# Turning P on two row tiles of 64 rows, both halves of an item in one go

## The chip, the cores and the metric

The kernel runs on one core of a Trainium2 chip. The metric is the device time of one execution in microseconds; of the kernel before, three executions were timed and their median counts. The profile and the trace come from one further execution, taken by the hardware profiler.

## The reference

A block of 16 sequences of 128 tokens with 128 features passes a small cross attention and then six layers of windowed self-attention and a gated feed-forward net. Nearly all of the time goes into the six layers. What matters of one layer, cut from the reference:

```python
def attn_layer(x, Wqkv, qs, ksc, Wo):
    q, k, v = jnp.split(x @ Wqkv, 3, -1)          # 16 heads of 64
    q, k = l2norm(q) * qs, l2norm(k) * ksc        # then a rotary turn of both
    ...
    sim = jnp.einsum('bhwie,bhwje->bhwij', bq, bk2) * QK_SCALE   # windows of 32, with the one before
    sim = jnp.where(mask, -jnp.finfo(sim.dtype).max, sim)
    attn = jax.nn.softmax(sim, -1)
    out = jnp.einsum('bhwij,bhwje->bhwie', attn, bv2)
    return out @ Wo

def ffn_layer(x, g, bln, W1, b1, W2, b2):
    xn = (x - mu) / jnp.sqrt(var + 1e-05) * g + bln
    a, gate = jnp.split(xn @ W1 + b1, 2, -1)
    return a * jax.nn.gelu(gate, approximate=False) @ W2 + b2

for i in range(DEPTH):                            # DEPTH = 6
    x = attn_layer(shift_tokens(x), ...) + x
    x = ffn_layer(shift_tokens(x), ...) + x
```

The kernel calls the softmax's result P. To multiply it with the values on TensorE, P has to be turned (its keys must lie on partitions); the result is PT.

## The kernel before

An item is one sequence in one layer: 6 x 16 = 96 items, worked in 48 pairs. Every engine has one instruction stream, written out by hand in its `step`, and `pipeline` (L176) repeats that for one pair after the other. One pass of the loop works on three pairs at once: `on(0)` is the newest pair (its products with Wqkv), `on(1)` the one before (scores, softmax, values, output projection), `on(2)` the oldest (the feed-forward net). The last argument of most steps is the item of the pair, r = 0 or 1. The order inside `step` is fixed, and an engine that waits holds up everything behind it.

PSUM has eight banks of 512 columns, and `BANK_USERS` (L202) writes out who uses which bank in which order. Before a product is written, `freed` (through `bank_left`, L237) lets TensorE wait until the readers of that bank's last user are done; `FREED` (L192) names the semaphores of those readers. Three of the eight lists touch the change:

```python
[("chunk", 1, 0, 0), ("up", 0, 0, 2), ("v", 1, 0, 0), ("chunk", 1, 1, 0)],                     # bank 0
[("chunk", 0, 0, 0), ("turn_p", 0, 0, 1), ("chunk", 2, 0, 0), ("chunk", 3, 1, 0), ...],        # bank 2
[("turn_qk", 1, 1, 1), ("turn_p", 1, 0, 1), ("values", 0, 0, 1), ("chunk", 2, 1, 0)],          # bank 6
```

So the product `v_chunk(1, 0, 0)` goes into the bank that `up(0, 2)` held, whose reader is `gelu` on ScalarE (semaphore `gelu_done`, three activations, L628); and `chunk(2, 0, 0)` goes into the bank of `turn_p(0, 1, 0)`, whose reader is the copy `p_out(0, 1, 0)` (L588).

P of one item lies in two halves of eight heads each (e = 0, 1), each 128 rows by 512 columns. `turn_p(e, lag, r)` (L1060) turns one half by four transposes of 128 x 128 through the helper `turn` (L1007 to L1010) into one bank; `PT_full[e]` tells ScalarE, which copies the bank to PT (`p_out`, L588) and sets `PT_ready[e]`; `values` (L1066 to L1080) waits for both halves. A half can be turned when `divide` on GpSimd (L413) has set `P_ready[e]`.

The order on TensorE around the two turns of item 0 is: `scores(0, 1, 1)`, `up(2, 2)`, `turn_p(0, 1, 0)`, `v_chunk(1, 0, 0)`, `turn_p(1, 1, 0)`, `chunk(3, 0, 0)`, `chunk(2, 0, 0)`, `values(1, 0)`, `down(2)`. Around those of item 1 it is: `down(2)`, `turn_p(1, 1, 1)`, `chunk(1, 0, 1)`, `turn_p(0, 1, 1)`, `chunk(3, 0, 1)`, `chunk(2, 0, 1)`, `values(1, 1)`. On ScalarE the order around the copies of item 0 is `gelu(2)` with a table load before and behind it, `p_out(0, 1, 0)`, `p_out(1, 1, 0)`, `split_high`, `exp(1, 1, 1)`, `exp(0, 1, 1)`. A `chunk` or `v_chunk` is three products of 512 columns (L1003 to L1005, `product`).

`values` runs on four tiles of 64 rows by 64 columns of the array and `scores` on eight tiles of 64 by 32; everything else in the loop uses the whole array. At the very end of the program 32 products on two row tiles of 64 by 128 turn the result back (L1206).

Of the kernel before, what the change touches and what calls it, by code (L numbers as in the profile page):

```python
# [31 lines left out]
def program(nc, x, ctxT, Wqkv, Wo, W1, W2, by_feature, every_token, shape_consts, out):  # L32
# [8 lines left out]
    def sem(name):  # L41
        return es.enter_context(nc.semaphore(name))

    with es:
# [15 lines left out]
        maskf, ident, centring, mean_of = (sc[:, 128 * i:128 * i + 128] for i in (2, 3, 4, 5))  # L60
# [25 lines left out]
        P = sb("P", [128, 2, 2, 8, DH])  # L86
        PT = sb("PT", [128, 2, 2, 512])
# [41 lines left out]
        def sems(name, n):  # L129
            return [sem(name + str(k)) for k in range(n)]  # L130
# [2 lines left out]
        SP_SEMS = [vs_full, wo_loaded, w2_loaded, w1_loaded]  # L133

        ch_full, v_full, qkT_full, sc_full = sems("ch_full", 4), sems("v_full", 2), sems("qkT_full", 4), sems("sc_full", 2)
        PT_full, up_full, pv_full = sems("PT_full", 2), sems("up_full", 3), sem("pv_full")
        Wo_full, xc_full, var_full, y_full = (sem(s) for s in ("Wo_full", "xc_full", "var_full", "y_full"))
        PE_SEMS = (ch_full + v_full + qkT_full + sc_full + PT_full + up_full + [pv_full, Wo_full, xc_full, var_full, y_full])

        rot_done, ss_done, t2_done = sems("rot_done", 4), sems("ss_done", 4), sems("t2_done", 4)  # L140
        mx_done, sc_out, sum_done, rs_done = sems("mx_done", 2), sems("sc_out", 2), sems("sum_done", 2), sems("rs_done", 2)
# [28 lines left out]
        wait_met = sem("wait_met")  # L170


        def n_(n):
            return n + START
# [59 lines left out]
        def bank_of(kind, k=0, r=0):  # L234
            return K[bank_place(kind, k, r)[0]]
# [236 lines left out]
        def _(act):  # L472
# [24 lines left out]
            with act.Fori(0, NB // PAIR) as pair:  # L497
# [23 lines left out]
                for j in range(2):  # L521
                    act.wait_ge(c_hT, pair * 2 + j + 1 + START)
                    act.sem_inc(wait_met, 1)
                    for g in range(2):
                        p = slice(64 * g, 64 * g + 64)
# [4 lines left out]
            def step(it, on, splitting):  # L530
# [50 lines left out]
                    ps = P[:, r, e].rearrange("p g c -> p (g c)")  # L581
                    nc.scalar.activation(ps, ps, ACT.Exp).then_inc(exp_done[e], 1)

                def p_out(e, lag, r):
                    n = (it - lag) * 2 + r
                    act.wait_ge(PT_full[e], n_(n) + 1)
                    act.wait_ge(pv_full, n_(n) - 1)
                    nc.scalar.copy(PT[:, r, e], bank_of("turn_p", e, r)[:]).then_inc(PT_ready[e], 1)  # L588

                def o_out(h, lag, r):  # L590
                    n = (it - lag) * 2 + r
# [113 lines left out]
        def _(dve):  # L705
# [68 lines left out]
            def step(it, on, splitting):  # L774
# [38 lines left out]
                def minus_maxima(e, lag, r):  # L813
                    n = (it - lag) * 2 + r
                    dve.wait_ge(mx_done[e], n_(n) + 1)
                    dve.wait_ge(PT_full[e], n_(n) - 1)
                    nc.vector.tensor_tensor(P[:, r, e], by_head(bank_of("scores", e, r)[:], 8), spread(nm[:, r, e], 8, DH),
                                            ALU.subtract).then_inc(sc_out[e], 1)

# [130 lines left out]
        def _(pe):  # L950
# [42 lines left out]
            def step(it, on, splitting):  # L993

                def freed(kind, k=0, r=0):

                    for readers, value in bank_left(it, kind, k, r):
                        pe.wait_ge(readers, value)
# [8 lines left out]
                def turn(bank, src, done):  # L1007

                    for t in range(4):
                        i = nc.tensor.transpose(bank[:, 128 * t:128 * t + 128], src[:, 128 * t:128 * t + 128], ident[:])  # L1010
                    i.then_inc(done, 1)
# [45 lines left out]
                                            stop=True, skip_group_check=True)  # L1057
                    i.then_inc(sc_full[s], 1)

                def turn_p(e, lag, r):  # L1060
                    n = (it - lag) * 2 + r
                    pe.wait_ge(P_ready[e], n_(n) + 1)
                    freed("turn_p", e, r)
                    turn(bank_of("turn_p", e, r), P[:, r, e].rearrange("p g c -> p (g c)"), PT_full[e])

                def values(lag, r):  # L1066
                    n = (it - lag) * 2 + r
# [84 lines left out]
                    scores(0, 1, 1)  # L1152
                if on(2):
                    up(2, 2)
                if on(1):
                    turn_p(0, 1, 0)
                if on(0):
                    v_chunk(1, 0, 0)
                if on(1):
                    turn_p(1, 1, 0)  # L1160
                if on(0):
                    chunk(3, 0, 0)
                    chunk(2, 0, 0)
# [1 line left out]
                    values(1, 0)  # L1165
                if on(2):
                    down(2)
                if on(1):
                    turn_p(1, 1, 1)
                if on(0):  # L1170
                    chunk(1, 0, 1)
                if on(1):
                    turn_p(0, 1, 1)
                if on(0):
                    chunk(3, 0, 1)
                    chunk(2, 0, 1)
# [97 lines left out]
```

## Time and profile before

| | us |
|---|---|
| median of 3 executions | 1595.66 |
| lowest, highest of them | 1594.83, 1598.72 |
| the profiled execution, its own time | 1600.49 |
| its span, first to last instruction | 1598.6 |
| TensorE busy in the span | 1506.6 |
| VectorE busy in the span | 1399.6 |
| ScalarE, GpSimd busy in the span | 1175.3, 1168.4 |

The span is what the trace covers; about 1.9 us of the execution's time lie around it. A product's start in the trace is the time at which it was handed to the array; where the weights are not there yet the columns stream later, so the start of the next product, less one product's length, is the better mark for when a product really began.

### The profile page before, as it was taken

What the parts mean: (1) busy time and instruction counts of PE and PEld (TensorE: products, weight loads), DVE (VectorE), ACT (ScalarE), POOL (GpSimd) and SP (SyncE); (2) the same over time, 40 slices, a digit from 0 to 9 for tenths busy, and PEclk for the clock granted to TensorE, in tenths of its full rate; (3) what the DMA queues carried; (4) which work ended last, traced back from release to release, by engine and by line L of the source; (5) the groups of instructions that cost most, each with busy time, mean ns of one, the idle gap of its engine ahead of it and who ended that gap; (6) DMA issues with size and microseconds to landing.
All of it is one profiled execution on the core that took longest, in us unless ns stands there. A gap on an engine that the chain in (4) does not pass through costs nothing.

```text
span 1598.6 us, 80227 instructions
## 1 busy us (share of the span) xinstructions
PE 1506.6 (94%) x31136; PEld 1251.0 (78%) x31136; DVE 1399.6 (88%) x2545; ACT 1175.3 (74%) x2333; POOL 1168.4 (73%) x1118
## 2 busy tenths in 40 slices
PE   4589999999999999999999999999999999999996
PEld 3367888888888888888888888888888888888875
DVE  3587899999999999989999999999999999999982
ACT  3456687788778778778877877877877777777772
POOL 1276777878877887787787788788778777777760
PEclk8689999999999999999999999999999999999996
DMA  5110011011110111101112110111110101000010
GB/s 144 42 44 28 28 36 42 26 49 58 31 36 26 42 39 57 41 26 36 42 29 68 29 38 29 33 42 61 36 35 20 30 25 62 29 20 30 20 30 28
DMA packets 41462, 62.40 MB, mean 39 GB/s; under 512 B 3662, under 2 KB 30412, under 8 KB 41420
## 3 DMA queue, kind: packets, MB, share of 16 engines
q1 hardware_dynamic: 41420, 61.84, 13.2%
q8 instruction: 27, 0.44, 0.1%
q14 instruction: 15, 0.12, 0.0%
HBM read 18.84 MB, written 1.05 MB: 12 GB/s over the span
## 4 chain that ended last, share of the span: by engine, by line
PE 86%; issue 4%; ACT 3%; DVE 2%; ACTq 1%; POOL 0%; DVEq 0%; POOLq 0%
PE bank L1010 13%; PE bank L1080 12%; PE bank L1092 10%; PE bank L1003 9%; PE bank L1053 8%; PE bank L1004 8%; PE bank L1005 8%; PE bank L1127 5%; PE bank L1116 3%; PE bank L1035 3%; PE bank L1117 2%; PE bank L1118 2%; ACT v L576 2%; DVE xng L841 1%; PE bank L1106 1%
## 5 line engine op out<-in xcount | busy, mean ns | idle before, releaser
L393 POOL TENSOR_TENSOR u<-u,t 128x512 f32<-128x512 f32 x384 | 498.2, 1308 | 40.5 <-DVE t L802 40.5
L407 POOL TENSOR_TENSOR u<-u,rn 128x512 f32<-128x512 f32 x384 | 401.8, 1068 | 78.8 <-ACT rn L556 78.8
L413 POOL TENSOR_TENSOR P<-P,rs 128x512 f32<-128x512 f32 x192 | 196.5, 1045 | 172.6 <-DVE rs L826 172.6
L1003 PE MATMUL bank<-Wl,xsh 128*128 (+1 forms) x576 | 273.4, 475 | 26.1 <-ACT v L576 22.7
L802 DVE TENSOR_TENSOR t<-bank,TS 128x512 f32<-128x512 f32 x384 | 258.0, 682 | 28.1 <-ACT sq L545 25.5
L793 DVE TENSOR_TENSOR u<-bank,TC 128x512 f32<-128x512 f32 x384 | 261.9, 682 | 6.0 <-ACT sq L545 3.1
L786 DVE TENSOR_REDUCE ss<-sq 128x8 f32<-128x512 f32 x384 | 250.5, 673 | 6.4 <-ACT sq L545 6.4
L1004 PE MATMUL bank<-Wh,xsl 128*128 (+1 forms) x576 | 228.5, 397 | 0.0
L1005 PE MATMUL bank<-Wh,xsh 128*128 (+1 forms) x576 | 228.0, 396 | 0.0
L545 ACT ACTIVATE sq<-bank 128x512 f32<-128x512 f32 x384 | 218.9, 598 | 5.8 <-PE bank L1005 5.3
L1010 PE MATMUL bank<-shape_constants,u 128*128 128x128 f32 x1536 | 219.2, 275 | 3.4 <-POOL u L407 3.2
L1010 PEld LDWEIGHTS bank<-shape_constants,u 128*128 128x128 f32 x1536 | 182.2, 141 | 34.9 <-POOL u L407 5.0
L562 ACT COPY qT<-bank 128x512 f32<-128x512 f32 x192 | 115.2, 600 | 122.3 <-PE bank L1010 121.1
L1080 PEld LDWEIGHTS bank<-PT,vs 64*64 64x64 f32 x6144 | 163.9, 135 | 37.5 <-issue 37.5
L1080 PE MATMUL bank<-PT,vs 64*64 64x32 f32 x6144 | 187.8, 220 | 3.0 <-ACT PT L588 3.0
L1080 PE MATMUL bank<-PT,v 64*64 64x32 f32 x6144 | 186.1, 219 | 2.6 <-issue 2.6
L1092 PE MATMUL bank<-OT,WoS 128*128 128x256 f32 x768 | 175.5, 382 | 1.2 <-ACT OT L594 1.2
L1080 PEld LDWEIGHTS bank<-PT,v 64*64 64x64 f32 x6144 | 164.7, 135 | 2.8 <-issue 2.8
L1003 PEld LDWEIGHTS bank<-Wl,xsh 128*128 128x128 f32 x576 | 109.5, 190 | 62.5 <-issue 55.7
L1092 PEld LDWEIGHTS bank<-OT,WoS 128*128 128x128 f32 x768 | 143.4, 192 | 19.2 <-issue 1.3
L1053 PEld LDWEIGHTS bank<-kT,qT 64*32 64x32 f32 x12288 | 123.3, 105 | 32.3 <-issue 32.3
L594 ACT COPY OT<-bank 128x512 f32<-128x512 f32 x192 | 109.1, 594 | 45.4 <-PE bank L1080 45.4
(102 smaller groups left out, 3040.0 us busy)
## 6 DMA issues: line engine op xcount, KB each, us to landing
vs<-v SPq DMA_DIRECT2D x96, 384.0 KB, 3.3
Wraw<-in_L_ffn_Wqkv_dram SPq DMA_DIRECT2D x72, 117.5 KB, 2.1
WoS<-in_L_ffn_Wo_dram SPq DMA_DIRECT2D x6, 512.0 KB, 3.7
W1h<-Wh SPq DMA_DIRECT2D x6, 341.0 KB, 2.5
W1l<-Wl SPq DMA_DIRECT2D x6, 341.0 KB, 2.9
Wraw<-in_L_ffn_W_dram SPq DMA_DIRECT2D x12, 116.0 KB, 2.2
OT<-in_x_dram SPq DMA_DIRECT2D x2, 512.0 KB, 5.6
v<-in_ctx_dram SPq DMA_DIRECT2D x2, 512.0 KB, 6.9
```

The source lines that it names most:

```text
L393: nc.gpsimd.tensor_tensor(u[:, r, c], u[:, r, c], t2[:, r, c % 2], ALU.add).then_inc(add_done[c], 1)
L407: nc.gpsimd.tensor_tensor(by_head(u[:, r, c]), by_head(u[:, r, c]), spread(rn[:, r, HC * c:HC * c + HC], HC, DH), ALU.mult).then_inc(qk_re ...
L786: nc.vector.tensor_reduce(ss[:, r, HC * c:HC * c + HC], by_head(square_out(c, r)), AX, ALU.add).then_inc(ss_done[c], 1)
L793: nc.vector.tensor_tensor(by_head(u[:, r, c]), by_head(bank_of("chunk", c, r)[:]), TC[:, layer(it - lag), c % 2].broadcast_to([128, HC, DH ...
L802: nc.vector.tensor_tensor(halves(t2[:, r, c % 2]), halves(bank_of("chunk", c, r)[:])[:, :, ::-1, :], TS[:, layer(it - lag), c % 2].broadca ...
L1003: nc.tensor.matmul(out, x[0], Wl[:, w], start=True, stop=False)
L1004: nc.tensor.matmul(out, x[1], Wh[:, w], start=False, stop=False)
L1005: nc.tensor.matmul(out, x[0], Wh[:, w], start=False, stop=True).then_inc(done, 1)
L1010: i = nc.tensor.transpose(bank[:, 128 * t:128 * t + 128], src[:, 128 * t:128 * t + 128], ident[:])
L1053: i = nc.tensor.matmul(bank_of("scores", e, r)[64 * w2 + 32 * a:64 * w2 + 32 * a + 32, at + (32 if w == 0 else 0):at + 64], qT[f, s, t, 32 ...
L1080: i = nc.tensor.matmul(bank_of("values", h, r)[64 * e:64 * e + 64, 64 * t + 32 * w2:64 * t + 32 * w2 + 32], (vs, v)[w2][p, r, head:head + ...
L1092: i = nc.tensor.matmul(bank_of("Wo")[:, 0:2 * S], WoS[:, k], OT[:, k].rearrange("p r s -> p (r s)"), start=(k == 0), stop=(k == INNER // 1 ...
```

## The change

The two calls of `turn_p` for an item become one. It waits for both halves of P and for both banks, and turns everything by sixteen transposes of 64 rows by 128 columns: rows 0 to 63 (g = 0) on the upper row tile of the array into one bank, rows 64 to 127 (g = 1) on the lower row tile into the other, the two alternating. One semaphore, `P_turned`, replaces the two of `PT_full`; `p_out(g)` waits for it and copies bank g, which now holds the 64 columns of g of all eight blocks, into every second run of 64 columns of PT. For item 0 the common turn stands behind `v_chunk(1, 0, 0)`, for item 1 behind `chunk(1, 0, 1)`; the turns that stood ahead of these products are gone.

```diff
-                def p_out(e, lag, r):
-                    n = (it - lag) * 2 + r
-                    act.wait_ge(PT_full[e], n_(n) + 1)
+                def p_out(g, lag, r):
+                    n = (it - lag) * 2 + r
+                    act.wait_ge(P_turned, n_(n) + 1)
                     act.wait_ge(pv_full, n_(n) - 1)
-                    nc.scalar.copy(PT[:, r, e], bank_of("turn_p", e, r)[:]).then_inc(PT_ready[e], 1)
+                    nc.scalar.copy(PT[:, r].rearrange("p e (t g i) -> p (e t) g i", g=2, i=64)[:, :, g],
+                                   bank_of("turn_p", g, r)[:].rearrange("p (k i) -> p k i", i=64)).then_inc(PT_ready[g], 1)
...
                 def minus_maxima(e, lag, r):
                     n = (it - lag) * 2 + r
                     dve.wait_ge(mx_done[e], n_(n) + 1)
-                    dve.wait_ge(PT_full[e], n_(n) - 1)
+                    dve.wait_ge(P_turned, n_(n) - 1)
...
-                def turn_p(e, lag, r):
-                    n = (it - lag) * 2 + r
-                    pe.wait_ge(P_ready[e], n_(n) + 1)
-                    freed("turn_p", e, r)
-                    turn(bank_of("turn_p", e, r), P[:, r, e].rearrange("p g c -> p (g c)"), PT_full[e])
+                def turn_p(lag, r):
+                    n = (it - lag) * 2 + r
+                    pe.wait_ge(P_ready[0], n_(n) + 1)
+                    pe.wait_ge(P_ready[1], n_(n) + 1)
+                    freed("turn_p", 0, r)
+                    freed("turn_p", 1, r)
+                    pe.sem_inc(wait_met, 1)
+                    for e in range(2):
+                        src = P[:, r, e].rearrange("p g c -> p (g c)")
+                        for t in range(4):
+                            for g in range(2):
+                                p, at = slice(64 * g, 64 * g + 64), 256 * e + 64 * t
+                                i = nc.tensor.transpose(bank_of("turn_p", g, r)[:, at:at + 64],
+                                                        src[p, 128 * t:128 * t + 128], ident[p, 64 * g:64 * g + 64])
+                    i.then_inc(P_turned, 1)
...
                 if on(2):
                     up(2, 2)
-                if on(1):
-                    turn_p(0, 1, 0)
                 if on(0):
                     v_chunk(1, 0, 0)
                 if on(1):
-                    turn_p(1, 1, 0)
+                    turn_p(1, 0)
                 if on(0):
                     chunk(3, 0, 0)
                     chunk(2, 0, 0)
...
-                if on(1):
-                    turn_p(1, 1, 1)
                 if on(0):
                     chunk(1, 0, 1)
                 if on(1):
-                    turn_p(0, 1, 1)
+                    turn_p(1, 1)
```

## Rows read from the trace of the kernel before

**Rows 1.** The page's busy times: engine, us, share of the span, instructions.

```profile
PE 1506.6 (94%) x31136; PEld 1251.0 (78%) x31136; DVE 1399.6 (88%) x2545; ACT 1175.3 (74%) x2333; POOL 1168.4 (73%) x1118
```

**Rows 2.** One steady stretch: length, busy PE, PEld, DVE, ACT, POOL, clock, DMA.

```profile
800.00:1000.00 200.00, 196.50 (x4174) 164.01 (x4167) 184.71 (x323) 154.43 (x306) 160.17 (x152) 1.00 0.13 40
```

**Rows 3.** TensorE's waits, longest total first: us in total, times, longest.

```profile
PE bank L1003 <- ACT v L576: 22.7, 46, 1.3
```

**Rows 4.** Time line around item 0's turns: start, length, engine, line, operation, tiles.

```profile
819.45 1.20 ACT L628 ACTIVATE gate<-bank,feature_columns 128x256 f32<-128x256 f32 x3
...
820.58 0.60 PE L1010 MATMUL bank<-shape_constants,P 128*128 128x128 f32 x4
...
821.25 0.40 PE L1004 MATMUL bank<-Wh,xsl 128*128 x1
...
821.72 0.60 PE L1010 MATMUL bank<-shape_constants,P 128*128 128x128 f32 x4
...
821.96 1.08 ACT L588 COPY PT<-bank 128x512 f32<-128x512 f32 x2
...
823.16 0.39 PE L1004 MATMUL bank<-Wh,xsl 128*128 x1
...
823.39 0.40 PE L1005 MATMUL bank<-Wh,xsh 128*128 x1
...
823.71 0.32 PE L1080 MATMUL bank<-PT,vs 64*64 64x32 f32 x8
```

**Rows 5.** What ScalarE waited for ahead of the gelu activations (L628): us, times.

```profile
  PE bank L1118: 2.4, 1
```

**Rows 6.** Time line of `chunk(0, 0, 0)` waiting for the copy of v.

```profile
813.20 0.56 ACT L576 COPY v<-bank 128x512 f32<-128x512 f32 x1
...
814.35 0.40 PE L1004 MATMUL bank<-Wh,xsl 128*128 x1
```

**Rows 7.** Groups by shape: line, engine, tile, columns, count, busy us, mean ns, idle.

```profile
L1003 PEld LDWEIGHTS bank<-Wl,xsh 128*128 128x128 f32 x576 | 109.5, 190 | 62.5 <-issue 55.7
...
L1080 PEld LDWEIGHTS bank<-PT,v 64*64 64x64 f32 x6144 | 164.7, 135 | 2.8 <-issue 2.8
...
L1010 PEld LDWEIGHTS bank<-shape_constants,P 128*128 128x128 f32 x768 | 94.5, 141 | 19.6 <-POOL P L413 1.2 <-issue 0.9
...
L1206 PEld LDWEIGHTS bank<-shape_constants,R 64*128 64x128 f32 x64 | 6.9, 329 | 2.0 <-issue 2.0
...
L1010 PE MATMUL bank<-shape_constants,P 128*128 128x128 f32 x768 | 115.9, 273 | 1.2 <-DVE u L793 0.6 <-POOL P L413 0.4 <-issue 0.2
...
L588 ACT COPY PT<-bank 128x512 f32<-128x512 f32 x192 | 110.1, 599 | 29.8 <-PE bank L1010 29.3
...
L594 ACT COPY OT<-bank 128x512 f32<-128x512 f32 x192 | 109.1, 594 | 45.4 <-PE bank L1080 45.4
```

**Rows 8.** Time line of TensorE from item 1's values back to the whole array.

```profile
801.19 0.30 PE L1080 MATMUL bank<-PT,vs 64*64 64x32 f32 x8
801.30 0.30 PE L1080 MATMUL bank<-PT,v 64*64 64x32 f32 x8
...
801.87 0.39 PE L1004 MATMUL bank<-Wh,xsl 128*128 x1
```

**Rows 9.** The program's last products, two row tiles: weight loads, then the stretch's clock.

```profile
1587.87 6.93 PEld L1206 LDWEIGHTS bank<-shape_constants,R 64*128 64x128 f32 x64 [1.97 <-issue]
...
1588.00:1594.00 6.00, 6.00 (x58) 6.00 (x58) 2.42 (x6) 0.00 (x0) 0.00 (x0) 0.50 0.26 72
```

**Rows 10.** Time line around item 1's turns; brackets: idle before, releaser.

```profile
825.52 2.04 POOL L413 TENSOR_TENSOR P<-P,rs 128x512 f32<-128x512 f32 x2
...
827.11 0.60 PE L1010 MATMUL bank<-shape_constants,P 128*128 128x128 f32 x4
...
828.25 0.60 PE L1010 MATMUL bank<-shape_constants,P 128*128 128x128 f32 x4
...
828.89 0.59 ACT L588 COPY PT<-bank 128x512 f32<-128x512 f32 x1 [0.44 <-PE bank L1010]
```

More of the change, by code:

```diff
@@ L135, in program @@
         ch_full, v_full, qkT_full, sc_full = sems("ch_full", 4), sems("v_full", 2), sems("qkT_full", 4), sems("sc_full", 2)
-        PT_full, up_full, pv_full = sems("PT_full", 2), sems("up_full", 3), sem("pv_full")
+        P_turned, up_full, pv_full = sem("P_turned"), sems("up_full", 3), sem("pv_full")
         Wo_full, xc_full, var_full, y_full = (sem(s) for s in ("Wo_full", "xc_full", "var_full", "y_full"))
-        PE_SEMS = (ch_full + v_full + qkT_full + sc_full + PT_full + up_full + [pv_full, Wo_full, xc_full, var_full, y_full])
+        PE_SEMS = (ch_full + v_full + qkT_full + sc_full + up_full + [P_turned, pv_full, Wo_full, xc_full, var_full, y_full])
         rot_done, ss_done, t2_done = sems("rot_done", 4), sems("ss_done", 4), sems("t2_done", 4)
```

## The prediction, made before the changed kernel was run

> **What bounds the kernel now.** I read the page first, then busy time by stretch, then TensorE's waits, then the time line of one pass. TensorE is the busiest engine of the span [rows 1]; in the steady state it is busy 98% of the time at the full granted clock, with VectorE at 92% behind it [rows 2]. Its only wait that comes back in every pass (46 times, 0.5 us each) is for ScalarE's copy of v ahead of `chunk(0, 0, 0)` [rows 3]. That wait hangs on work that TensorE itself started late in the pass before, so whatever time TensorE loses around the turns comes back in full in the period, and so does what it gains. The change has to be read at two places: around item 0's turns and around item 1's.
>
> At item 0 the reader is to see how tightly two things meet [rows 4]. `up(2, 2)` ends at 820.58 and the turn of half 0 fills 820.58 to 821.02. Behind it comes `v_chunk(1, 0, 0)`, whose bank is freed by gelu; gelu's three activations end at 819.45 + 1.20 = 820.65. ScalarE is late there by its own queue, not by TensorE: it waited for TensorE ahead of gelu in one pass out of 48 [rows 5]. From the end of a ScalarE instruction to the product that waited for it I count 0.36 us: v's copy ends at 813.20 + 0.56 = 813.76, and the second product of that chunk starts at 814.35, so the first really began 0.23 earlier, at 814.12 [rows 6]; and `chunk(2, 0, 0)` begins at 823.16 - 0.23 = 822.93, behind a copy to PT that ends at 821.96 + 0.59 = 822.55 [rows 4]. (0.23 is one product of 512 columns, 823.16 to 823.39 [rows 4].) So today `v_chunk(1, 0, 0)` could not begin before 820.65 + 0.36 = 821.01; it begins at 821.25 - 0.23 = 821.02. The turn of half 0 lies wholly in the cover of gelu and costs nothing.
>
> **The change, part by part.** *What the turns cost TensorE.* Four transposes take (0.60 - 0.27) / 3 = 0.109 us each from start to start [rows 4, 7], 0.43 for a half, 0.87 for an item.
>
> *What the new turn costs.* It has a price at each end that the old one has not, since the array is used in another tiling. Going in: the last product before item 0's values has streamed at 823.39 + 0.23 = 823.62, and the first of the values starts at 823.71, 0.09 later [rows 4]; then its own weights must be loaded. Coming out: the last eight of the values start at 801.30, their second batch of four 0.06 later, and some 0.05 after that it has streamed, at about 801.42; the next product really begins at 801.87 - 0.23 = 801.64 [rows 8]. That is 0.2, of which half is a weight load that nothing covers.
> Between the ends the trace has no transposes on row tiles, so I bound a pair of them, one on each tile. Loads of 64 and 128 columns last 135 and 190 ns, hence some 110 ns of loading for 128 columns, an estimate; a transpose's load lasts 141 ns, 50 less, hence some 55 ns [rows 7]. Its stream is half of the 107 ns of a full one, 53. The last products of the program have the new shape: 64 loads of 0.33 in 6.93 us, hence (6.93 - 0.33) / 63 = 0.105 from one to the next, at clock 0.50 [rows 7, 9]; a pair takes 0.21 there and would take 0.105 at full clock. That is what a load of 110 ns with the stream hidden behind it gives, and also what a load and a stream of 53 ns each, one behind the other, give. I take the first reading, since there the values agree (eight of them start some 0.116 after the eight before, that is four tiles every 0.058, which is their loading time of 0.055 with the stream hidden [rows 7, 8]); with a transpose's shorter load a pair takes 0.058. The upper bound is 0.107, the lower 0.053, the stream alone.
> Sum: 0.09 and 0.05 for the first load in, 7 x 0.058 + 0.053 = 0.46 stream, 0.20 out: 0.80 instead of 0.87. So the row tiles halve the streaming and the two ends take the gain back, but for 0.07 an item.
>
> *What the new place costs at item 0.* With the turn of half 0 gone from ahead of it, `v_chunk(1, 0, 0)` still can't begin before 821.01: TensorE idles for 0.43 where it used to turn. The chunk ends at 821.71, as before. Now all of P is still to be turned, not one half: the stream runs from 821.85 to 822.31, and `chunk(3, 0, 0)` from 822.51 to 823.21. `p_out` of the first bank, which before began at 821.96 [rows 4], now waits for the whole turn: from the end of a turn's stream (828.25 + 4 x 0.109 = 828.69) to the copy (828.89) it is 0.20 [rows 10], so it runs from 822.51 to 823.10, and `chunk(2, 0, 0)`, which needs that bank, begins 0.36 later, at 823.46, and ends at 824.16. Before, it ended at 823.62. Loss: 0.54 us a pass. The second copy ends at 823.58, in time for `values`. Queued behind the copies on ScalarE are the weight split and item 1's exponentials; they move by the same 0.54 as TensorE does, and GpSimd's division after them.
>
> *At item 1* the common turn stands behind `chunk(1, 0, 1)`, 0.70 after `down`, at 827.81, and wants both halves; the second is divided at 825.52 + 2.04 = 827.56 [rows 10]. TensorE needs 0.25 to 0.4 from there to the first load (the 0.36 above, less a load, plus more waits to step through), so between nothing and 0.1 is lost against the 0.07 gained: I take nought. Its copies are later by some 0.2 than the second of today, but `values` stands two chunks behind, which covers them.
> Two edits I put at nothing: the copy to PT, strided from now on, since the copy of the values' bank, which is strided in the same way, takes 594 ns against 599 [rows 7]; and the other semaphore for `minus_maxima`, since P's buffer of the pair before was turned a pass ago.
>
> *Sum.* 46 of the passes have gelu and a new pair's chunk at once (48 pairs, two passes apart): 46 x 0.54 = 24.8, item 1 nought: about +25 us. The profiled execution took 1600.5, so 1625.5 on it; it lies 4.8 above the median, and on the median the forecast is 1595.7 + 25 = 1621 us.
>
> **The rivals.** *Load and stream of a row tile come one behind the other.* A pair then takes 0.107 at full clock. For it: the program's last products fit it as well; against it: the values' rate. Item 0's stream is 0.80 long, its loss 0.89; item 1 loses 1.14 - 0.87 = 0.27. 46 x 0.89 + 48 x 0.27 = 54: 1650 us.
> The Trainium skill says in "TensorE: Matmul & The Clock Gate", section "Part 3: Packing small matmuls — row/col tiling", that a weight load overlaps with products in flight only when the row group differs, which is this rival; the rows bear it out no better than the other reading.
>
> *The two row tiles don't work at once*, so that the change doesn't do what it says: sixteen times 0.058 is a stream of 0.93; item 0 loses 1.0, item 1 0.40: 46 + 19 = 65, 1661 us. Against it: the side-by-side rate of the program's last products.
>
> *Not slower: the ends cost nothing for this tiling.* Both ends were read on tiles of 64 by 64; tiles of 64 by 128 keep the columns of the whole array, and could be entered without a gap and with the next load covered. Then a turn is 0.46: item 0's stream ends at 822.17, its copy at 822.96, `chunk(2, 0, 0)` at 824.02, a loss of 0.40; item 1 gains 0.41. 46 x 0.40 - 48 x 0.41 = -1: 1594 us. It decides once the ends together cost under 0.1; a shorter handover to ScalarE would then make it faster.
> The Trainium skill, in "TensorEngine Tiling (Array Packing)", section "Key Properties", says that a change of tiling mode drains the engine, which speaks against this rival; the 0.09 ahead of the values [rows 4] agrees for theirs, and no row shows it for this one.
>
> **How the numbers follow.** Forecast as worked out (1612 to 1632, by item 1's term and 0.1 in the handover): 0.60. Ends at about half their price (1601 to 1611): 0.09. Load behind stream: 0.13. No concurrency: 0.04. Free ends: 0.14, of which 0.08 within 0.3% and 0.06 faster. A difference under 0.3% (4.8 us) can hardly be told from none. So faster 0.06, same 0.08, slower 0.86. The range runs from 1605 to 1652: it holds the forecast, half of the half-priced ends and the serial load, 0.78, and a little beyond each bound.
>
> **What would show it.** In the trace of after: TensorE idle for 0.4 us between `up(2, 2)` and `v_chunk(1, 0, 0)`, released by gelu (L628); sixteen transposes of 64 x 128 in about 0.46 us from first to last; a gap ahead of `chunk(2, 0, 0)` released by the copy to PT (L588); item 0's values 0.54 later after `up` than now, item 1's about as late as now. I am wrong if `v_chunk(1, 0, 0)` starts right behind `up(2, 2)`, if the transposes take 0.8 or more, or if the gap ahead of the values stays what it was.

## The result, and the profile after

The changed kernel takes 1638.1 us (median of 4 executions, 1634.5 to 1640.3), the kernel before 1596.2 (4 executions, 1594.8 to 1598.7): 1.0258 times as long, 95% interval 1.0236 to 1.0281. The prediction was 1621 with a range of 1605 to 1652: the sign and the range held, the size did not (25 us against 42). That the range held is luck: the forecast's own band ended at 1632, and the range reached to 1652 for the sake of a rival, load and stream one behind the other, which the trace below rules out.

The steady stretch comes first: length, then busy PE, PEld, DVE, ACT, POOL, clock and DMA, as in [rows 2].

```profile
800.00:1000.00 200.00, 195.93 (x4286) 157.59 (x4285) 183.50 (x326) 153.72 (x302) 154.40 (x147) 1.00 0.14 41
```

It tells nothing of a loss: TensorE is about as busy as before. The length of a row reaches beyond the stream (0.28 for a product of `up` that streams 0.12), so that the short times in which TensorE stands idle hide behind the row ahead of them. The time has to be read from starts. This is the time line around item 0's turn (start, length, engine, line, operation; brackets: idle before and its releaser). The helper's lines are now L1004 to L1006, the turn L1073, the values L1091.

```profile
833.19 1.20 ACT L629 ACTIVATE gate<-bank,feature_columns 128x256 f32<-128x256 f32 x3
...
834.20 0.28 PE L1129 MATMUL bank<-xfh,W1h 128*128 128x256 f32 x1
...
834.64 0.49 PE L1004 MATMUL bank<-Wl,xsh 128*128 x1 [0.17 <-issue]
...
834.98 0.39 PE L1005 MATMUL bank<-Wh,xsl 128*128 x1
...
835.20 0.39 PE L1006 MATMUL bank<-Wh,xsh 128*128 x1
...
835.52 0.57 PEld L1073 LDWEIGHTS bank<-shape_constants,P 64*128 64x128 f32 x16 [0.35 <-issue]
835.52 0.71 PE L1073 MATMUL bank<-shape_constants,P 64*128 64x64 f32 x16
...
836.27 1.07 ACT L588 COPY PT<-bank 128x512 f32<-128x512 f32 x2 [0.59 <-PE bank L1073]
836.50 0.39 PE L1005 MATMUL bank<-Wh,xsl 128*128 x1
...
837.44 0.40 PE L1005 MATMUL bank<-Wh,xsl 128*128 x1
...
838.00 0.32 PE L1091 MATMUL bank<-PT,vs 64*64 64x32 f32 x8
```

Five things are to be seen, with products of 0.23 as in the prediction.

- `up(2, 2)` has streamed at 834.20 + 0.12 = 834.32, and `v_chunk(1, 0, 0)` really begins at 834.98 - 0.23 = 834.75: TensorE stands idle for 0.43, until 0.36 after gelu's end (833.19 + 1.20 = 834.39).
- The chunk has streamed at 835.20 + 0.23 = 835.43; the first load of the turn follows 0.09 later.
- The sixteen loads take 0.57 from the first start to the last end, one of them 0.139, and the two of a pair start within 0.01 of each other: (0.57 - 0.139) / 7 = 0.062 from pair to pair.
- The turn has streamed at 836.06 (its last product starts at 836.01 and streams for 0.05); `chunk(3, 0, 0)` really begins at 836.50 - 0.23 = 836.27. The whole turn, from the chunk ahead of it to the one behind, is 836.27 - 835.43 = 0.84.
- The copies begin at 836.27; the first of the two takes 0.59, as in [rows 7], and ends at 836.86; `chunk(2, 0, 0)` really begins at 837.44 - 0.23 = 837.21, 0.35 after that and 0.24 after `chunk(3, 0, 0)` has ended. The brackets call such waits "issue"; by their times it is the copy.

From gelu's end to the values it is 838.00 - 834.39 = 3.61; before it was 823.71 - 820.65 = 3.06 [rows 4]. Item 1's turn, same columns:

```profile
840.66 1.04 POOL L413 TENSOR_TENSOR P<-P,rs 128x512 f32<-128x512 f32 x1
...
841.63 0.40 PE L1005 MATMUL bank<-Wh,xsl 128*128 x1
...
842.19 0.71 PE L1073 MATMUL bank<-shape_constants,P 64*128 64x64 f32 x16
...
842.95 1.07 ACT L588 COPY PT<-bank 128x512 f32<-128x512 f32 x2 [0.70 <-PE bank L1073]
843.17 0.39 PE L1005 MATMUL bank<-Wh,xsl 128*128 x1
```

`chunk(1, 0, 1)` has ended at 841.40 + 0.70 = 842.10, and the next chunk really begins at 842.94: again 0.84 to 0.85 for the turn. P was divided at 841.70, in time.

The values of item 0 come again one pass later:

```profile
869.15 0.32 PE L1091 MATMUL bank<-PT,vs 64*64 64x32 f32 x8
```

A pass lasts 869.15 - 838.00 = 31.15 here (median of the passes in the first loop 31.18) against 30.64 before: 0.54 more.

*Where the 42 us are.* The start of item 0's values in each of the 48 passes, subtracted from the next, gives every pass its length in both traces. The difference of the two spans is 1632.7 - 1598.6 = 34.0 us:

| stretch | after less before, us |
|---|---|
| passes in the two loops but for the first of the second loop | 21.1 |
| the first passes (written out) and first round of the first loop: 36.1, 34.3, 32.8 against 32.3, 36.7, 30.7 | 3.5 |
| first pass of the second loop: 33.54 against 30.95 | 2.6 |
| from the values of the loops' last pass to the program's end (the last passes are written out again) | 6.8 |

The first line is the loss that was forecast. The last three are passes whose instructions run for the first time, and the prediction has no term for them. The medians differ by 41.9; the other 8 us lie between executions: after's profiled one is its fastest, 3.6 below its median, and before's lies 4.3 above its own.

In after's last pass the values stop in their midst (TensorE alone):

```profile
1587.23 0.48 PE L1091 MATMUL bank<-PT,v 64*64 64x32 f32 x8
1587.44 0.40 PE L1091 MATMUL bank<-PT,vs 64*64 64x32 f32 x2
...
1589.95 0.33 PE L1091 MATMUL bank<-PT,vs 64*64 64x32 f32 x3 [2.11 <-issue]
1589.97 0.31 PE L1091 MATMUL bank<-PT,v 64*64 64x32 f32 x1
```

Both operands had been there for the products ahead of the stop, so it waits for no data. In the same pass the scores stop in their midst as well:

```profile
1582.61 0.42 PE L1054 MATMUL bank<-kT,qT 64*32 64x64 f32 x21 [1.57 <-issue]
```

What moves in those stretches are fetches of instructions. The DMA view of 100 to 200 us, 1300 to 1360 and 1560 to 1630 shows, one line each (packets, MB, share):

```profile
q8 instruction: 16, 0.26, 1.0%
...
q8 instruction: 5, 0.08, 0.5%
...
q8 instruction: 6, 0.10, 0.6%
```

These 27, and one at 68 us, are all that the page counts, 16 KB each; between 200 and 1300 us, in the rounds of the first loop, there is none. The page of after has 28, that of before 27:

```profile
q8 instruction: 28, 0.46, 0.1%
```

The change writes 32 more instructions (16 loads and 16 products) into every pass on TensorE. That they cost time where they are fetched was a theory at this point.

### The profile page after: what moved, and what is told of

It is laid out like the page before. It is cut to its first block, busy times and chain, and to the rows that moved or that the text cites. A ratio compares the mean times of both kernels' runs of the same rounds, so it can differ in the third digit from the quotient of the medians.

```text
span 1632.7 us, 81762 instructions
## 1 busy us (share of the span) xinstructions
PE 1524.3 (93%) x31904; PEld 1225.4 (75%) x31904; DVE 1403.0 (86%) x2545; ACT 1171.0 (72%) x2333; POOL 1167.3 (71%) x1118
## 4 chain that ended last, share of the span: by engine, by line
PE 85%; issue 4%; ACT 2%; DVE 2%; ACTq 1%; POOL 0%; DVEq 0%; POOLq 0%
PE bank L1091 12%; PE bank L1004 11%; PE bank L1103 10%; PE bank L1054 8%; PE bank L1011 8%; PE bank L1005 7%; PE bank L1006 7%; PE bank L1138 5%; PE bank L1073 4%; PE bank L1127 3%; PE bank L1036 3%; PE bank L1128 2%; PE bank L1129 2%; ACT v L576 2%; PE bank L1117 1%
## 5 line engine op out<-in xcount | busy, mean ns | idle before, releaser
L1004 PE MATMUL bank<-Wl,xsh 128*128 (+1 forms) x576 | 283.5, 492 | 31.9 <-ACT v L576 22.2
L1006 PE MATMUL bank<-Wh,xsh 128*128 (+1 forms) x576 | 228.1, 396 | 0.0
L1091 PEld LDWEIGHTS bank<-PT,vs 64*64 64x64 f32 x6144 | 165.6, 135 | 43.6 <-issue 43.6
L1091 PE MATMUL bank<-PT,vs 64*64 64x32 f32 x6144 | 189.9, 221 | 7.8 <-issue 4.7
L1091 PE MATMUL bank<-PT,v 64*64 64x32 f32 x6144 | 188.6, 220 | 6.1 <-issue 6.1
L1004 PEld LDWEIGHTS bank<-Wl,xsh 128*128 128x128 f32 x576 | 108.7, 189 | 93.0 <-issue 79.3
L1091 PEld LDWEIGHTS bank<-PT,v 64*64 64x64 f32 x6144 | 166.5, 136 | 5.4 <-issue 5.4
L588 ACT COPY PT<-bank 128x512 f32<-128x512 f32 x192 | 103.3, 590 | 68.5 <-PE bank L1073 68.5
```

Of the source, the lines that this page charges most:

```text
L1004: nc.tensor.matmul(out, x[0], Wl[:, w], start=True, stop=False)
L1006: nc.tensor.matmul(out, x[0], Wh[:, w], start=False, stop=True).then_inc(done, 1)
L1091: i = nc.tensor.matmul(bank_of("values", h, r)[64 * e:64 * e + 64, 64 * t + 32 * w2:64 * t + 32 * w2 + 32], (vs, v)[w2][p, r, head:head + ...
```

## The experiments

Theories. A, the prediction's: item 0 loses by its place (gelu's cover is gone) and by the handover through one semaphore, and the row tiles by themselves gain a little. B: the row tiles cost more than was worked out. C: what the steady passes don't explain is code that is fetched during the run.

**The place without the tiles.** Before, with both halves turned by whole-array transposes at the new places, and two semaphores as before:

```diff
-                if on(1):
-                    turn_p(0, 1, 0)
                 if on(0):
                     v_chunk(1, 0, 0)
                 if on(1):
+                    turn_p(0, 1, 0)
                     turn_p(1, 1, 0)
...
-                if on(1):
-                    turn_p(1, 1, 1)
                 if on(0):
                     chunk(1, 0, 1)
                 if on(1):
+                    turn_p(1, 1, 1)
                     turn_p(0, 1, 1)
```

> The kernel before with nothing but the new place: both halves of P are turned behind v_chunk(1, 0, 0) and behind chunk(1, 0, 1), by the eight transposes on the whole array, each half with its own semaphore as before. Theory (place): v_chunk waits for gelu with nothing to cover the wait, and chunk(2, 0, 0) waits for the first copy to PT, which here may start after the first half. From the rows of before, the first copy starts at 822.35 instead of 821.96 and chunk(2, 0, 0) ends 0.38 us later, item 1 is unchanged: a steady pass of 30.64 + 0.38 = 31.02 us, some 17 us on the whole, 1614 us. Rival (tiles): the loss of the change comes from the row tiles and their changes of tiling, and the place costs nothing: 30.64 us a pass, 1596 to 1600 us.

Measured: 1611.3 against 1596.8, ratio 1.0091 (1.0064 to 1.0118); a pass lasts 31.00. The copies begin halfway through the turn:

```profile
825.68 0.39 PE L1005 MATMUL bank<-Wh,xsh 128*128 x1
...
825.91 1.04 PE L1010 MATMUL bank<-shape_constants,P 128*128 128x128 f32 x8
826.54 1.07 ACT L588 COPY PT<-bank 128x512 f32<-128x512 f32 x2 [0.39 <-PE bank L1010]
```

The place alone loses 0.36 a pass, as expected (0.38): the 0.43 of standing, less most of the 0.08 that TensorE waited ahead of `chunk(2, 0, 0)` before (822.62 + 0.23 = 822.85 to 822.93).

**The place and the one semaphore.** As above, and each copy waits for both halves:

```diff
-                    act.wait_ge(PT_full[e], n_(n) + 1)
+                    act.wait_ge(PT_full[0], n_(n) + 1)
+                    act.wait_ge(PT_full[1], n_(n) + 1)
```

> As the kernel with the new place and whole-array transposes, and besides each copy to PT waits for both halves, as the single semaphore of the change makes it. Theory (place and handover): the stream of the whole-array turn ends at 822.58, the first copy starts at 822.78 and chunk(2, 0, 0) ends 0.81 later than before; item 1 is covered by its two chunks: 31.45 us a pass, +37 us, 1633 us. That would be 0.27 a pass more than the changed kernel (31.18 us), by which its row tiles would be a gain at item 0. Rival (tiles): 1596 to 1600 us. A second thing is told apart: the changed kernel lost 24 us in its steady passes and some 9 more in the passes that are written out, where it has 32 more weight loads and products each; this kernel has none more, so its loss should be its steady loss alone.

Measured: 1644.8, ratio 1.0302 (1.0270 to 1.0334); a pass lasts 31.61, which is 0.97 more than before and 0.61 more than with two semaphores. The expectation of 31.45 was low because item 1 loses too: from item 0's values to item 1's it is 6.61 against 6.47. The chunks behind item 1's turn do not quite cover both copies if these begin only at the end of 0.87. The changed kernel differs from this one by the tiles and is 0.43 a pass shorter (31.18). So B falls: within the new order the row tiles gain. The gain is more than the 0.03 between the two turns, since coming out of the tiles (0.21) lies behind the stream, where the copies don't wait for it:

```profile
842.10 1.03 PE L1011 MATMUL bank<-shape_constants,P 128*128 128x128 f32 x8
...
843.22 1.07 ACT L589 COPY PT<-bank 128x512 f32<-128x512 f32 x2 [0.87 <-PE bank L1011]
```

Here the copies begin 843.22 - 842.10 = 1.12 after the chunk ahead of the turn has ended, in the changed kernel 0.84.

**The tiles under gelu's cover.** After, with item 0's turn ahead of `v_chunk(1, 0, 0)`:

```diff
-                if on(0):
-                    v_chunk(1, 0, 0)
                 if on(1):
                     turn_p(1, 0)
                 if on(0):
+                    v_chunk(1, 0, 0)
+                if on(0):
                     chunk(3, 0, 0)
```

> The changed kernel with one edit: item 0's common turn stands ahead of v_chunk(1, 0, 0) instead of behind it, so that it lies in the cover of gelu again. It has to wait for the second half of P, divided at 820.68, so it streams from about 821.05 to 821.54 and v_chunk begins at 821.75 instead of 821.02; the copies to PT are then early enough for chunk(2, 0, 0). Theory (cover): item 0 loses 0.23 instead of 0.55 a pass, item 1 keeps its gain of 0.05: 30.82 us a pass; with the 9 us of the passes that are written out, 1596 + 8 + 9 = 1613 us. Rival (tiles): where the turn stands makes no difference, 31.2 us a pass, 1638 us.

Measured: 1613.9, ratio 1.0113 (1.0087 to 1.0140); a pass lasts 30.63, that of before 30.64. The steady loss is gone, all of it, where 0.23 at item 0 were expected to stay: the turn's stream was put 0.37 behind the division of P's second half, and in the trace its first load starts 0.07 behind it (821.18 + 2.04 = 823.22; the profile's ends on GpSimd are rough). The first copy waits for the table load behind gelu:

```profile
821.18 2.04 POOL L413 TENSOR_TENSOR P<-P,rs 128x512 f32<-128x512 f32 x2 [3.20 <-DVE rs L827]
...
823.22 1.28 ACT L632 ACT_TABLE_LOAD   x1
823.29 0.61 PEld L1073 LDWEIGHTS bank<-shape_constants,P 64*128 64x128 f32 x16 [0.21 <-issue]
...
824.51 1.08 ACT L588 COPY PT<-bank 128x512 f32<-128x512 f32 x2
...
825.48 0.39 PE L1004 MATMUL bank<-Wl,xsh 128*128 x1
```

The first of these copies ends 0.59 later, at 825.10, and with 0.36 for the handover `chunk(2, 0, 0)`, whose first product is the L1004 at 825.48, is just not held up. But the kernel is still 17 us slower than before: theory C has to explain that, since A and B speak of steady passes only.

**The tiles at item 1 alone.** Before, with item 1's turn on row tiles (`turn_p_tiles`, the changed kernel's `turn_p` with one semaphore for each bank) behind `chunk(1, 0, 1)`:

```diff
-                if on(1):
-                    turn_p(1, 1, 1)
                 if on(0):
                     chunk(1, 0, 1)
                 if on(1):
-                    turn_p(0, 1, 1)
+                    turn_p_tiles(1, 1)
```

> Item 0 is turned as before, at its two old places on the whole array; item 1 is turned as in the change, on two row tiles behind chunk(1, 0, 1). Theory: item 1's turn is worth 0.05 us a pass, 30.59 us, 2.4 us on the whole, and half of the added code in the passes that are written out costs some 4: 1598 us, between 1593 and 1602. Rival (tiles): half of the loss of the change, 1616 us or so.

Measured: 1605.5, ratio 1.0060 (1.0042 to 1.0079), above the expected 1593 to 1602, although a pass is 0.06 shorter (30.58). So the tiles do gain in the loop, and by the medians 11 us are lost outside the steady passes.

**The same in the loops alone**, the written-out passes as before:

```diff
                 if on(1):
-                    turn_p(0, 1, 1)
+                    if isinstance(it, int):
+                        turn_p(0, 1, 1)
+                    else:
+                        turn_p_tiles(1, 1)
```

> Item 1 is turned on two row tiles as in the kernel with item 1 alone, but only in the two loops; in the five passes that are written out it is turned as before, so that they hold not one instruction more for TensorE. Theory (code): the 9 us that the kernel with item 1 alone lost, though its steady pass was 0.06 shorter, went into the written-out passes, where TensorE's instructions are fetched while they run; without the added ones the total follows the steady pass, 45 x 0.06 = 2.7 us less than before, 1594 us, but for the first pass of each loop. Rival: the loss comes from something else that the row tiles do in every pass or at the ends, and stays: 1605 us.

Measured: 1600.9 (12 executions), ratio 1.0028 (1.0012 to 1.0044); a pass lasts 30.61, 0.03 longer than with the same code everywhere. That lies between the theory and its rival. With the new code only in the loops, which still run for the first time once each, about half of the loss outside the steady passes is left.

**Only more code.** Before, with one more instruction of TensorE's sequencer (a semaphore that nobody waits for is raised) behind each product of `product`, in the written-out passes alone; 36 more in each of the three that call it, and no other work:

```diff
+                    more = isinstance(it, int)
                     nc.tensor.matmul(out, x[0], Wl[:, w], start=True, stop=False)
+                    if more:
+                        pe.sem_inc(wait_met, 1)
```

> The kernel before, with one semaphore increment behind each product of chunk and v_chunk in the written-out passes alone: 36 more instructions a pass for TensorE's sequencer, no work for the array, and each behind a product of 0.23 us that covers it. The change adds 32 a pass. Theory (code): the written-out passes get longer by their fetches, 5 to 15 us in all, 1602 to 1612 us, with the steady pass at 30.64. Rival: code is fetched ahead and costs nothing: 1596 us.

Measured: 1608.7, ratio 1.0069 (1.0045 to 1.0093); a pass in the loop as before (30.65). Its last pass, whose own code is unchanged, now stops in the midst of the values too:

```profile
1560.24 0.28 PE L1087 MATMUL bank<-PT,vs 64*64 64x32 f32 x3
1562.46 0.32 PE L1087 MATMUL bank<-PT,vs 64*64 64x32 f32 x3 [1.94 <-issue]
```

More instructions, no work, 13 us by the medians: theory C has its direct evidence. That a stop of 2 us turns up in a pass whose instructions did not change suggests that it counts where the bounds of the fetched blocks fall, as well as how many blocks there are; no run moved the bounds alone.

**Both items early, in the loops alone**: the second and third experiment's better halves, row tiles for item 0 under gelu's cover and for item 1 behind `chunk(1, 0, 1)`, written-out passes as before.

```diff
                 if on(1):
-                    turn_p(0, 1, 0)
+                    if isinstance(it, int):
+                        turn_p(0, 1, 0)
+                    else:
+                        turn_p_tiles(1, 0)
                 if on(0):
                     v_chunk(1, 0, 0)
-                if on(1):
+                if on(1) and isinstance(it, int):
                     turn_p(1, 1, 0)
```

> As the kernel with item 0's turn ahead of v_chunk(1, 0, 0) and both items on row tiles, but only in the two loops; the five written-out passes are as before. That kernel had a steady pass of 30.63 us, no longer than before, and yet took 18 us more in all. Theory (code): the 18 us are the fetches of the added instructions in the written-out passes; without them some 6 us stay for the first pass of each loop, as with item 1 alone in the loops: 1601 us, and 30.63 us a pass. Rival: the 18 us are something else, 1614 us.

Measured: 1606.0 (10 executions), ratio 1.0054 (1.0037 to 1.0071); a pass lasts 30.62. That is 5 above the theory and 8 below the rival: taking the new code out of the written-out passes saves about half of the loss, and in the traces all of that in the first passes; the late ones lose as much as with the new code everywhere (in the ledger below 10.4 against 9.2).

**Whole-array turns of item 0 both ahead of `v_chunk(1, 0, 0)`, and the tiles for item 1**, in the loops alone for the tiles:

```diff
                     turn_p(0, 1, 0)
+                    turn_p(1, 1, 0)
                 if on(0):
                     v_chunk(1, 0, 0)
-                if on(1):
-                    turn_p(1, 1, 0)
```

> As the kernel with item 1 on row tiles in the loops, and besides item 0's two halves, on the whole array as before, both stand ahead of v_chunk(1, 0, 0). The second half of P is divided at 820.68 and its turn begins at 821.01, so it need not wait; the copies to PT are ready earlier, and the wait of 0.08 ahead of chunk(2, 0, 0) goes. Theory (cover and handover): 30.58 - 0.08 = 30.50 us a pass, some 6 us less than before in all, 1590 us. Rival: TensorE's own work is all that counts, which the order does not change: 30.58 us, 1594 us.

Measured: 1599.5 (12 executions), ratio 1.0015 (1.0002 to 1.0028); a pass lasts 30.60, 0.10 more than expected. It is the best of the variants and no better than the kernel before. The 0.08 was not gained: the whole turn is through earlier, but the copies still begin when the table load behind gelu ends (814.73 + 1.28 = 816.01), as in the kernel before (820.67 + 1.28 = 821.95, copy at 821.96):

```profile
814.64 1.03 PE L1014 MATMUL bank<-shape_constants,P 128*128 128x128 f32 x8
814.73 1.28 ACT L635 ACT_TABLE_LOAD   x1
...
816.03 1.07 ACT L589 COPY PT<-bank 128x512 f32<-128x512 f32 x2
...
817.19 0.40 PE L1008 MATMUL bank<-Wh,xsl 128*128 x1
```

`chunk(2, 0, 0)` really begins at 817.19 - 0.23 = 816.96, 0.34 after the first copy's end (816.03 + 0.59 = 816.62).

**Without gelu's table loads** (gelu becomes the identity), before and after:

```diff
-                    nc.scalar.preload_act_table(ACT.Gelu)
...
-                        i = nc.scalar.activation(gate[0:w, t], up_out(GATE, t), ACT.Gelu,
+                        i = nc.scalar.activation(gate[0:w, t], up_out(GATE, t), ACT.Identity,
...
-                    nc.scalar.preload_act_table_set("natural_log_exp_and_others")
```

> The kernel before with gelu replaced by the identity and the two table loads around it left out, so that ScalarE ends gelu some 1.3 us earlier and is free for the copies to PT some 2.6 us earlier. To be compared with the changed kernel under the same edit. Both theories: the turn of half 0 takes TensorE's time now as before, only the wait of 0.08 ahead of chunk(2, 0, 0) goes: 30.56 us a pass.

> The changed kernel with gelu replaced by the identity and the two table loads around it left out, so that gelu has ended before up(2, 2) has. The kernel before under the same edit has a steady pass of 30.66 us. Theory (cover): v_chunk(1, 0, 0) follows up(2, 2) at once, as if from 820.58 on; the turn's stream ends at 821.92, the first copy to PT at 822.72, and chunk(2, 0, 0) ends at 823.77 instead of 823.62: 0.15 lost at item 0, 0.05 won at item 1, some 30.76 us a pass, of the 0.54 that the change costs with gelu in place. Rival (tiles): the 0.54 stays, 31.2 us a pass.

Measured, one execution each: before 1594.6 with a pass of 30.66, after 1621.8 with a pass of 30.83. The changed order now loses 0.17 a pass, not 0.54. In after's variant `v_chunk(1, 0, 0)` starts right behind `up(2, 2)`, which has streamed at 829.18 + 0.12 = 829.30, and only the wait for the copy is left ahead of `chunk(2, 0, 0)`:

```profile
829.18 0.28 PE L1127 MATMUL bank<-xfh,W1h 128*128 128x256 f32 x1
829.30 0.39 PE L1002 MATMUL bank<-Wl,xsh 128*128 x1
...
830.85 1.07 ACT L588 COPY PT<-bank 128x512 f32<-128x512 f32 x2 [2.45 <-PE bank L1071]
831.07 0.39 PE L1003 MATMUL bank<-Wh,xsl 128*128 x1
...
832.01 0.39 PE L1003 MATMUL bank<-Wh,xsl 128*128 x1
```

`chunk(3, 0, 0)` has ended at 831.07 - 0.23 + 0.70 = 831.54, `chunk(2, 0, 0)` really begins at 832.01 - 0.23 = 831.78: 0.24, less the 0.03 and 0.05 that the tiles gain at the two turns, comes to the 0.17 within 0.01. So gelu's cover is 0.37 of the 0.54, and the handover, less what the tiles gain, the rest.

The variant of before missed its expectation (30.56). The wait for v's copy, the one that bounds the period, has grown in it (TensorE's waits: total, times, longest; the kernel before has 22.7 in 46, [rows 3]):

```profile
PE bank L1001 <- ACT v L576: 24.8, 45, 1.3
```

24.8 / 45 = 0.55 a pass against 22.7 / 46 = 0.49: of the 0.10 that lie between the pass expected and the pass measured, 0.06 were waited for there.

**The ledger of the code theory.** For each trace, less that of before: the steady passes of both loops, and the two late stretches that hold code running for the first time, that is the first pass of the second loop and from the loops' last values to the end. The first passes are left out, since before's own trace has one of 36.7 there where five of the six variants with no code added in them have 31.6 to 33.4. The last two columns are explained below the table.

| kernel | code added on TensorE | steady passes, us | late first-run stretches, us | fetches | stops in these stretches, us | half clock in them, us |
|---|---|---|---|---|---|---|
| place, two semaphores | none | 14.8 | 0.1 | 27 | 0 | 0.2 |
| place, one semaphore | none | 40.9 | 0.3 | 27 | 0 | -3.3 |
| before without table loads | none | 0.7 | -2.2 | 27 | 0 | -3.1 |
| tiles at item 1, loops alone | 16 a pass | -1.6 | 3.9 | 27 | 3.2 | -1.3 |
| whole turns early, tiles at item 1, loops alone | 16 a pass | -2.0 | 4.9 | 27 | 3.2 | 1.5 |
| tiles at item 1 | 16 a pass | -2.2 | 9.1 | 28 | 3.6 | 11.0 |
| tiles early, loops alone | 32 a pass | -0.5 | 10.4 | 28 | 4.5 | 12.3 |
| tiles early | 32 a pass | 0.2 | 9.2 | 28 | 4.8 | 13.6 |
| after | 32 a pass | 21.1 | 9.4 | 28 | 5.8 | 10.2 |
| after without table loads | 32 a pass | 6.6 | 9.5 | 28 | 4.9 | 14.0 |
| only more code | 36 in each of three passes | 0.4 | 11.3 | 28 | 6.7 | 13.5 |

The three kernels with no code added lose nothing there; two with a little lose 4 to 5; all six with a 28th fetch lose 9 to 11, whatever they do in the loop. The last line is the plainest: its instructions are all added in the first three passes, and the late stretches, where its code is that of before, lose most. That the added code costs this time is shown.

The traces also show how. *Stops for a fetch.* In the twelve traces TensorE stops 66 times for more than 0.6 us in the midst of the values or the scores, and every time it goes on 1.19 to 1.58 us after a packet of the instruction queue q8 has ended. In after the packet ahead of the stop of 2.11 runs from 1587.00 to 1588.39, and the values go on at 1589.95; in the kernel with only more code it runs from 1559.78 to 1561.11, and they go on at 1562.46. Before has three such stops as well, all of them in its first passes; this is the first:

```profile
120.66 0.24 PE L1080 MATMUL bank<-PT,v 64*64 64x32 f32 x1 [1.15 <-issue]
```

*The clock.* The six kernels that lose 9 to 11 run 10 to 14 us longer at half of TensorE's clock in these stretches, the others do not. In after the granted clock is 0.50 through the second half of item 0's values and `down` of the last pass, and a second time from the middle of item 1's values on; before goes through both items' values of that pass at full clock. One stretch of each, after first (length, busy PE, PEld, DVE, ACT, POOL, clock, DMA):

```profile
1587.00:1593.80 6.80, 4.69 (x86) 3.91 (x78) 1.57 (x5) 0.61 (x2) 2.04 (x2) 0.50 0.03 6
1558.00:1566.00 8.00, 6.29 (x268) 5.72 (x261) 2.58 (x7) 3.21 (x7) 2.05 (x2) 1.00 0.02 5
```

`down` in after, in a steady pass and in the last one:

```profile
840.00 1.57 PE L1138 MATMUL bank<-hT,W2S 128*128 128x256 f32 x6
...
1591.38 2.77 PE L1138 MATMUL bank<-hT,W2S 128*128 128x256 f32 x6
```

In the 12 us before the clock fell at 1587.0, TensorE had stood idle three times for 1.5 to 1.6 us, and one of these times was the stop in the scores; before stood idle there twice, for 1.6 and 1.9, and its clock falls only at 1566.6, behind item 1's values. So a stop may cost more than its own length. That the added stops bring the earlier fall about is not shown: two kernels with 3.2 us of stops have no more half clock than the others without added code, one with 3.6 has 11 us, and no run changed the clock by itself.

What was not settled is how a single pass's share comes about (where the bound of a fetched block falls): it would need versions with the same code at shifted places. Nor is the loss of the first passes settled: after's are 5 to 9 us longer than those of the five variants named above, rather than the 3.5 by which they exceed before's, but an unchanged first pass varies by 5 us from trace to trace.

## Why the prediction was right or wrong

- *Gelu's cover.* Right: TensorE stands for 0.43 until 0.36 behind gelu, as worked out. Letting gelu end before `up(2, 2)` took away 0.37 of the 0.54.
- *The turn on row tiles.* Right within 0.04: 0.84 against 0.80. Going in took 0.09 and coming out 0.21, as read from the values; a pair took 0.062, not 0.058. The rival of load and stream one behind the other (0.107) fell: the load's share of 0.055, an estimate, and the stream's of 0.053 fit into 0.062 only if one hides the other. The rival of no concurrency (0.93 of stream) and that of free ends fell too: the ends are 0.35 of the 0.84. The Trainium skill says in "TensorE: Matmul & The Clock Gate", section "Part 3: Packing small matmuls — row/col tiling", that a weight load overlaps with products in flight only where the row group differs; for this form the measured 0.062 does not agree with that.
- *The handover.* Right: copies 0.21 after the stream, `chunk(2, 0, 0)` 0.35 after the first copy, item 0's values 0.55 later (forecast 0.54).
- *Item 1.* Taken at nought, it gained 0.03 to 0.06 a pass (0.03 with item 1 alone on tiles in the loops, 0.06 with it everywhere), inside its bounds. The second experiment shows how near the cover of two chunks was: with 0.87 of whole-array turns in place of 0.84, and all copies behind them, it costs 0.14.
- *The count.* 46 times 0.54 was a little much: the later passes of the second loop lose 0.35 each, and the loops come to 21 rather than 24.8.
- *The missing term.* This is the step that failed. "46 x 0.54 = 24.8, item 1 nought" treats the passes that are written out as if they were rounds of the loop, and puts the 768 products and 768 loads that the change adds at the time of their streams alone. They are instructions as well, and where code runs for the first time they cost 9.4 us in the late stretches and 3.5 in the first passes, 13 us by the two profiles: TensorE stops for fetches in the midst of its rows, and in the late stretches it runs 10 us longer at half clock. The steady passes lost 21 of the 24.8 forecast, so the excess over the forecast lies in these passes and in the 8 us between executions. The cause could be seen in before's trace, which has the same queue with 27 fetches and three stops of 1.1 to 1.4 us behind them.
- *"Whatever time TensorE loses comes back in full in the period, and so does what it gains."* The first half held: 0.55 lost around the turn, 0.54 in the period. The second did not. Without the table loads, 0.06 of what item 0 gained was waited for at v's copy instead. With the whole turns early nothing was gained at all, since the copy to PT waits for the table load and not for the turn. Behind TensorE's chain there is a second one through ScalarE, gelu, table load, copy to PT, `chunk(2, 0, 0)`; in the kernel before it is the longer one there, by 0.08.

## What to carry to other kernels

Before two steps are joined, ask what each of them was covering: here the first half of a turn filled the 0.43 us that TensorE would have stood for gelu, and joining it to the second half moved it out from under that cover and delayed the copy that frees the next bank, though the joined step itself was no slower. Count instructions as well as streams: splitting products into small tiles in a kernel whose passes are partly written out adds code, and code that runs once was paid for here with stops of 0.6 to 2.1 us and with stretches at half clock among them. A cheap test for either is an edit that changes the place without the tiles, and one that adds instructions without work.

## What was unexpected of the hardware

- Instructions are fetched during the run in blocks of 16 KB, nearly all of them where code runs for the first time (in five of the twelve traces one block comes in a later round of the first loop), and TensorE can stop for it in the midst of a row of small products: 2.11 us in after, 1.94 in the kernel that has only 108 sequencer instructions more. All 66 such stops end 1.19 to 1.58 us after a fetch.
- The late passes of the kernels with a 28th fetch run 10 to 14 us longer at half clock than those of before; in after the products of `down` take 2.77 there in place of 1.57.
- Sixteen transposes of 64 rows by 128 columns, alternating between two row tiles, follow each other at 0.062 us a pair, hardly over the 0.053 that one of them streams; of their loads only the first lies open. The change of tiling at both ends (0.14 up to the first stream, 0.21 out) takes nearly all of that back: 0.84 for sixteen, against 0.87 for eight on the whole array.
